# A coupling network's half exchange: DMAs into a swapped copy, or products that read one half and write the other

## What is computed

```
out = x                                    # x: 8 sequences of 512 tokens, 128 channels
for _ in range(3):
    tf = coupling_net(out)                 # 128 -> 128 -> 64 -> 32 -> 1, gelu, sigmoid
    combined = 0.7 * gf + 0.3 * tf         # gf: one number for each sequence
    coupling = 0.1 + adaptive_range * (combined - 0.5) * 2.0
    o_r, o_i, p_r, p_i = split(out, 4)     # by channels, 32 each
    out = out + coupling * concat([p_r, -p_i, -o_r, o_i])
```

## Time and profile before

| | us |
|---|---|
| median of 3 runs | 1001.28 |
| lowest, highest | 998.72, 1004.40 |
| the profiled execution | 1009.27 |
| its span, from first to last instruction | 1007.4 |

### The profile page before, as it was taken

The page is one execution under the profiler, slowest core; times in us unless marked ns, Lnnn a source line. Parts: engine busy times, 40 slices in busy tenths (PEclk is TensorE's granted clock), DMA queues, the critical chain, the costliest instruction groups (busy, mean ns, idle before and its releaser), DMA issues. The chain is left out here.

```text
span 1007.4 us, 18361 instructions
## 1 busy us (share of the span) xinstructions
PE 898.3 (89%) x6656; PEld 459.4 (46%) x6656; DVE 691.9 (69%) x1038; ACT 646.2 (64%) x1408; POOL 371.8 (37%) x369
## 2 busy tenths in 40 slices
PE   4699999999999999969989989498779999999996
PEld 2233434344444344438878878122233444444443
DVE  7769898998989999503333358477766767766653
ACT  4458677778777878843323226575477778877874
POOL 4011010224343332004655644464564547544200
PEclk9569899999999999989999999699799999999999
DMA  7632526050404000026666553139997999999700
GB/s 222 247 147 87 200 78 231 24 186 23 173 24 172 27 27 20 7 67 198 203 194 207 161 173 92 42 69 144 153 107 76 112 106 103 102 101 115 85 12 21
DMA packets 80957, 114.30 MB, mean 113 GB/s; under 512 B 12930, under 2 KB 57988, under 8 KB 78436
## 3 DMA queue, kind: packets, MB, share of 16 engines
q1 hardware_dynamic: 73668, 94.87, 47.4%
q0 software_dynamic: 6352, 17.86, 5.3%
q10 hardware_dynamic: 848, 0.40, 0.1%
HBM read 56.00 MB, written 33.57 MB: 89 GB/s over the span
## 5 line engine op out<-in xcount | busy, mean ns | idle before, releaser
L916 DVE TENSOR_REDUCE a_nmax<-quad 128x2 f32<-128x1024 f32 x256 | 302.6, 1220 | 32.5 <-PE quad L527 29.8
L726 ACT ACTIVATE a_probs<-bank 128x512 f32<-128x512 f32 x339 | 191.0, 598 | 55.2 <-PE bank L544 36.7
L1840 ACT ACTIVATE a_late<-quad 128x256 f32<-128x256 f32 (+3 forms) x512 | 180.4, 461 | 40.1 <-PE quad L1650 39.3
L556 PE MATMUL av<-a_probs,a_va 128*32 128x256 f32 x2048 | 167.5, 400 | 0.9 <-ACT a_probs L726 0.6
L1963 DVE SCALAR_TENSOR_TENSOR a_late<-a_late,const 128x512 f32<-128x512 f32 x128 | 117.1, 923 | 74.2 <-ACT a_late L1840 73.9
L527 PE MATMUL quad<-k_stack,q_stack 24*128 24x512 f32 x512 | 133.4, 524 | 9.9 <-DVE a_nmax L916 5.7
L544 PE MATMUL bank<-q_stack,k_stack 26*128 26x512 f32 x339 | 138.0, 505 | 4.5 <-DMA q_stack<-a_nparts 2.7
L726 ACT ACTIVATE a_probs<-misc 128x512 f32<-128x512 f32 x173 | 103.3, 597 | 26.3 <-PE bank L544 17.2
L1243 POOL DMA_INDIRECT expert_rows<-m_ob,m_xr x78 | 75.7, 971 | 116.3 <-DVE m_ob L1393 95.6
L1650 PE MATMUL quad<-q_stack,k_stack 96*128 96x256 bf16 (+3 forms) x512 | 104.3, 306 | 7.2 <-ACT a_late L1840 3.5
L440 POOL DMA_INDIRECT sorted_rows<-x_rows,a_slot x64 | 62.4, 976 | 105.6 <-PE av L556 103.1
(11 more groups left out here) (278 smaller groups left out, 1381.9 us busy)
## 6 DMA issues: line engine op xcount, KB each, us to landing
m_wu<-packed_weights SPq DMA_DIRECT2D x39, 384.0 KB
spread<-a_parts SPq DMA_DIRECT2D x48, 256.0 KB
q_stack<-a_parts SPq DMA_DIRECT2D x96, 128.0 KB, 7.3
k_stack<-a_parts SPq DMA_DIRECT2D x96, 128.0 KB, 7.8
q_stack<-spread SPq DMA_DIRECT2D x7, 1024.0 KB
k_stack<-spread SPq DMA_DIRECT2D x7, 1024.0 KB
sorted_rows<-in_shape_constants POOLq DMA_DIRECT2D x5, 1040.0 KB, 5.4
m_xr<-sorted_rows SPq DMA_DIRECT2D x39, 130.0 KB
```

The lines of the kernel that those rows point to most:

```text
L556: last = pe.matmul(av[STRIP * j:STRIP * (j + 1), at], va[b % 2][:, kt, GH * j + c, :], probs[:, (GH * s + j) % 8, at], start=(kt == 0 and ...
L726: act.activation(probs[:, (GH * s + j) % 8, :], col_bank(n)[:, :], ACT.Exp, scale=scale).then_inc(col_free, 1)
L916: dve.tensor_reduce(nmax[quad % 2][:, at:at + 2 * TT:TT], row_slot(n)[:, :, :], AX_X, ALU.max, negate=True)\
L1840: act.activation(probs[:, (64 * b + n) % 12, kt * P:T], quad[:, n % 4, kt * P:T], ACT.Square, bias=1.0, scale=0.25)\
```

## The change

SyncE no longer exchanges halves. VectorE makes the product in two instructions, each on 64 partitions: it reads coupling and value of one half of the channels and writes the delta of the other half. The sign vector is turned, since a factor now stands on the partitions that are read and not on those that are written. The stacks of batch 0 are issued at once when their splits are done. EARLY is (0, 1), (2), (3), (4), (5), (6), (7) where it was (0, 1), (2), (3), (), (4), (5), (6, 7). `values(0, 0)` moves from the start of the attention into the last round of the coupling, in front of its layer 4.

```diff
-    sign = np.ones((P, 1), np.float32)
-    sign[C // 4:3 * C // 4] = -1.0
+    sign = -np.ones((P, 1), np.float32)
+    sign[C // 4:3 * C // 4] = 1.0
...
-        EARLY = ((0, 1), (2,), (3,), (), (4,), (5,), (6, 7))
+        EARLY = ((0, 1), (2,), (3,), (4,), (5,), (6,), (7,))
...
-            def swap(n):
-                t = n % B
-                wait_now(sp, n)
-                wait(sp, delta_done, n - GROUP + 1)
-                sp.dma_start(swapped[0:D2, t, :], now(n)[D2:C, :]).then_inc(swap_in[n % GROUP], 16)
-                sp.dma_start(swapped[D2:C, t, :], now(n)[0:D2, :]).then_inc(swap_in[n % GROUP], 16)
-
-            for n in range(ALL):
-                swap(n)
-                if B <= n < B + 2 * len(PAIRS):
-                    half, row = divmod(n - B, len(PAIRS))
-                    stack(0, 0, half, (row,))
+            stack(0, 0, 0)
+            stack(0, 0, 1)
             stack(1, 1, 0)
             stack(1, 1, 1)
...
                 if k >= 1:
                     layer3(k - 1)
+                if not more:
+                    wait(pe, lay[0], ALL)
+                    values(0, 0)
...
-            wait(pe, lay[0], ALL)
-            values(0, 0)
             for i in range(B):
                 main(i, i % 2, i)
...
             def product(n):
-                t = n % B
                 wait(dve, coupled, n + 1)
-                dve.wait_ge(swap_in[n % GROUP], 32 * (n // GROUP + 1))
+                wait_now(dve, n)
                 wait(dve, updated[n % 2], n // 2)
-                dve.tensor_tensor(delta[n % 2], coup[n % 2], swapped[:, t, :], ALU.mult).then_inc(delta_done, 1)
+                for to, of in ((slice(0, D2), slice(D2, C)), (slice(D2, C), slice(0, D2))):
+                    last = dve.tensor_tensor(delta[n % 2][to, :], coup[n % 2][of, :], now(n)[of, :], ALU.mult)
+                last.then_inc(delta_done, 1)
```

More of the change, by code:

```diff
@@ L1483, in second_layer @@
         xc = S["s"]
-        swapped = xc[:, :, :].rearrange("p (b t) c -> p b (t c)", b=B)
         half = sb("half", [P, 5])
@@ L1507, in second_layer @@
         lay = [sem(f"layer{i}") for i in range(4)]
-        swap_in = [sem(f"swap_in{i}") for i in range(GROUP)]
         coupled, delta_done = sem("coupled"), sem("delta_done")
```

## The result

The changed kernel takes 1009.67 us (median of 8 runs, 1008.29 to 1013.24); the kernel before, beside it, 1001.24 (8 runs, 998.72 to 1004.95). The ratio is 1.0081, with an interval of 1.0060 to 1.0103: slower by 6 to 10 us. The forecast was 1010.9.

What follows compares the result with a forecast made beforehand. VectorE's work plus GpSimd's, taken in turns, was held to bound the coupling stage. Exchange removal -7.2, halves +18.2 and stage end -1.4 gave +9.6 us on the median of 1001.28: 1010.9 us, range 1002 to 1017.

Steps and rivals of the forecast that it cites:

- What bounds the stage: Coupling stage: VectorE binds even without DMA stalls; removing the exchange DMAs gains 7.2 us, 62.4 against 69.6.
- The engines take turns: Coupling stage: VectorE and GpSimd instructions with both inputs in SBUF hold each other off, so their work adds up.
- The price of the halves: VectorE's products in the coupling stage: 24 more instructions at 0.68 us a half cost 18.2 us over six groups.
- The lower end: Half products on VectorE following each other by 0.60 us, with overlap: 14.4 us in six groups.
- The sum: At the attention's first weighting: -7.2 + 18.2 - 1.4 = +9.6 us, bounds +5.8 and +11.6.
- Rival (a), half a cost: VectorE's half products: time goes with partitions, so a half costs half; 992.7 us, chance 0.06.
- Rival (b), made up in batch 0: Attention's batch 0 gives back its 6.4 us excess over batch 1: +3.2, 1004.5 us; chance 0.17.
- Rival (c), the clock: TensorE falls to 1.2 GHz in the coupling loop, its slack hiding about half: +4, 1015 us; chance 0.13.
- The prediction's own sign of being wrong: Coupling loop: a granted TensorE clock below 0.9 was listed among the signs that the forecast is wrong.
- SyncE's queue: Batch 0's stacks go out when their splits are done; attention's first scores do not end on them, so nothing taken.

Runs made afterwards that it cites:

- One_straight: Changed kernel with one product of 128 partitions on its own lanes in place of the two halves, exchange left out of the computation; ratio 0.9912 to the kernel before.
- odd_on_vector: Changed kernel with GpSimd's update of the odd tile done by VectorE, right behind that of the even tile; ratio 1.0058 to the kernel before.
- folded_split: Changed kernel without couplings (folded into product and update), half products reordered, all updates and the stage's splits on VectorE; ratio 0.9954 to the kernel before.
- Two_straight: Changed kernel with two 64-partition products per tile that stay on their own lanes, exchange left out of the computation; ratio 1.0111 to the kernel before.
- by_halves: Changed kernel with a pair's half products reordered: first half of both tiles, then second half of both; ratio 1.0109 to the kernel before.
- before_rest: Kernel before, exchange DMAs and whole products kept, with only the new EARLY order and the values ahead of the last layer 4; ratio 1.0127 to the kernel before.

## Why the prediction held, point by point

**What bounds the stage.** Right. The chain put a quarter of 100 us on the exchange DMAs; their going, with the moved chunks and values, brought 8.9. The number came from the groups that had no stall: 9.52 + 5 x 10.58 us. One_straight has 10.5 us for a group.

**The engines take turns.** Right, and it carries the result: odd_on_vector and folded_split put work on the full engine and made it faster.

**The price of the halves.** The mechanism was right, the size a little low. The term was 18.2 us, with 14.4 and 20.2 as its ends; it measures 20.2 (86.23 - 66.04), the upper end. The step is 0.70 us and not 0.68, and the first half of a pair is held too, behind the coupling: the forecast had counted the other halves and the update, but not that one. A quiet pair pays 5.45 - 3.68 = 1.77 us (673.25 - 669.57 = 3.68 in one_straight), where 1.60 stood. The lower end was right for what it stood for: 24 instructions without alternation cost 14.2.

**The sum.** +9.6 at the first weighting was forecast, +11.3 came: 2.0 from the halves, less 0.3 from a larger gain. The measured medians say +8.4 (6 to 10). What stands behind the stage doesn't explain the difference: from the first coupling to the end of the span it is 355.6 us after and 344.7 and 343.8 in the two profiles of the kernel before, +10.9 to +11.8. Two_straight and by_halves, which have the changed kernel's stage within 0.7 us, measured +1.1% by the ratio; their medians lie 8.8 and 8.7 us above that of the kernel before. So about 2 us stay open. That the forecast time fell within 1.3 us of the median is partly luck: two errors of 1 to 3 us cancel, and the second is not settled.

**Rival (a), half a cost.** Out: 64 x 512 lasts 0.69 us, like 128 x 512. The row of 16 partitions had said so.

**Rival (b), made up in batch 0.** Out. Batch 0 takes 37.40 us instead of 39.04, 1.6 of the 6.4, but the second profile of the kernel before has 38.24 there, and 1.2 us is lost again behind it: from the first weighting to the end of the span it is 269.3 us after, and 269.7 and 269.0 in the two profiles of before.

**Rival (c), the clock.** It fell, as the rival said, and cost nothing, which the rival had not. Groups 1, 3, 4 and 5 have granted clocks of 0.75, 0.88, 0.88 and 0.64. The prediction's own sign of being wrong, a clock below 0.9 in the loop, came without the loss that it stood for. The same line in group 1 and in group 2:

```profile
665.79 3.23 PE L1720 MATMUL bank<-coupled,net_w 128*128 128x512 f32 x4 [2.16 <-DVE coupled L2046]
...
679.68 2.27 PE L1720 MATMUL bank<-coupled,net_w 128*128 128x512 f32 x4
```

After 2.16 us without a matmul layer 1 of two tiles takes 3.23 us, where at full clock it takes 2.27, and TensorE is busy for 13.72 of the 13.88 us of group 1. Group 2 with a clock of 1.00 is 13.87 us long. TensorE fills its slack with slower work, and no wait of VectorE of 653 to 736 us is put down to it. I had let its slack hide half.

**SyncE's queue.** The forecast took nothing for it. The time was right and the reason incomplete: before_rest shows a wait of 12.36 us that appears as soon as the chunks move and the stacks don't. I looked at who waits for the stacks' results and not at who waits to write into their source.

**What stays open.** Why the whole time grew by some 2 us less than the stage, why the stages ahead of the coupling end anywhere within 16 us with the same code, and whether the order of the chunks is worth +0.7 or -0.7 us in the changed kernel.

## What to carry to other kernels

A chain of waits names what came last, not what its going is worth: look for a stretch of the same loop in which the stall doesn't occur, and take its length. Where two engines hold each other off, work belongs on the one that does it in less time, even if that one is full; their sum is the bound. Before a DMA is replaced by instructions of a full engine, see whether other DMAs can leave the queue: here that gave 0.4% where the replacement lost 0.8%.

## What the runs showed of the hardware

- VectorE and GpSimd: with both inputs in SBUF a product of 0.68 us takes 1.6 beside GpSimd's operations, and each operation of GpSimd 1.33 to 2.0 instead of 1.16. A cast with one input takes 1.50 instead of 0.42. Moving 12 updates from GpSimd to VectorE shortened the stage by 5.1 us.
- VectorE's instructions of 512 columns step by 0.60 us on the same partitions and by 0.70 when the start partition changes, at 64 partitions as at 128. No price of reading one half and writing the other shows: four halves take 2.80 us either way.
- TensorE's clock fell to 1.2 GHz after 2.16, 2.13 and 1.92 us without a matmul, in front of groups 1, 3 and 4. Group 2 had no such gap in front of it, TensorE being still busy with the slowed work of group 1, and after its own gap of 1.11 us the clock stayed at 2.4 GHz. A drop is not a loss where the engine has slack.
- An exchange of 128 KB landed after 7.5 us in the median with 24 other DMAs of that size among the exchanges, and after 3.9 when twelve of them were issued ahead.
